# Another order for the small jobs inside an attention stage on one Trainium2 core

## What is computed

```python
x = x + 0.5 * ffn(layernorm(x))          # silu(x Wg) * (x Wu), then Wd; hidden size 768
x = x + attention(layernorm(x))          # 16 heads of 16, bias -slope * |i - j|, softmax, Wo, bo
x = x + 0.5 * ffn(layernorm(x))
```

## Time and profile before

| | |
|---|---|
| median of 3 runs | 894.81 us (894.04 to 895.18) |
| the profiled execution | 898.4 us; its span from first to last instruction 896.6 us |
| PE, PEld | busy 825.1 (92%), 503.3 us |
| DVE, ACT, POOL | busy 647.6 (72%), 522.5 (58%), 426.2 us (48%) |
| largest groups | DVE row maxima 328.5 us in 512 instructions; ACT exponentials 259.9 us in 256; POOL multiplications 186.8 us in 256 |

### The profile page before, as it was taken

The page is one execution under the profiler, slowest core; times in us unless marked ns, Lnnn a source line. Parts: engine busy times, 40 slices in busy tenths (PEclk is TensorE's granted clock), DMA queues, the critical chain, the costliest instruction groups (busy, mean ns, idle before and its releaser), DMA issues.

```text
span 896.6 us, 13035 instructions
## 1 busy us (share of the span) xinstructions
PE 825.1 (92%) x4576; PEld 503.3 (56%) x4576; DVE 647.6 (72%) x1359; ACT 522.5 (58%) x745; POOL 426.2 (48%) x486
## 2 busy tenths in 40 slices
PE   2999999858899999999999999999899987999997
PEld 2788888724354454453453444444443436888886
DVE  6898878567767777777777777776778715777764
ACT  4444434414667677777677677777577774344443
POOL 0444433422644654744644745645555545344443
PEclk9999999966999999999999999999799999999999
DMA  9320000283532532541531540540522000010001
GB/s 360 112 31 3 2 3 3 33 109 39 72 46 29 72 47 28 72 54 20 72 54 20 72 64 13 69 67 15 65 44 29 2 1 2 26 48 26 26 26 48
DMA packets 21491, 43.17 MB, mean 48 GB/s; under 512 B 3849, under 2 KB 5913, under 8 KB 21209
## 3 DMA queue, kind: packets, MB, share of 16 engines
q1 hardware_dynamic: 21400, 41.92, 27.3%
HBM read 12.02 MB, written 4.62 MB: 19 GB/s over the span
## 4 chain that ended last, share of the span: by engine, by line
PE 64%; DVE 21%; issue 4%; DMA 4%; ACT 3%; SPq 1%; POOL 1%; DVEq 0%; ACTq 0%
PE ps L938 60%; DVE row_max L859 7%; DVE hid L755 3%; DMA q_aug<-max_row 3%; PE ps L994 2%; ACT stage L612 2%; PE ps L950 1%; DVE xn L717 1%; DVE xnt L877 1%; DVE newton L694 1%; ACT xnt L618 1%; DVE var L686 1%; SPq L406 1%; DMA k_aug<-parts 1%; DVE mean_var L676 1%
## 5 line engine op out<-in xcount | busy, mean ns | idle before, releaser
L859 DVE TENSOR_REDUCE row_max<-ps 128x1 f32<-128x512 f32 x512 | 328.5, 684 | 117.6 <-PE ps L938 116.3
L650 ACT ACTIVATE probs<-ps 128x1024 f32<-128x1024 f32 x256 | 259.9, 1026 | 44.6 <-PE ps L938 44.1
L531 POOL TENSOR_TENSOR probs<-probs,diag 128x256 f32<-128x256 f32 x256 | 186.8, 734 | 199.3 <-ACT probs L650 199.1
L466 POOL TENSOR_TENSOR hid_r<-hid,hid_r 128x512 fp32r<-128x512 f32 x96 | 125.2, 1305 | 178.5 <-ACT hid_r L558 177.3
L938 PE MATMUL ps<-xnt,wgu_r 128*128 128x512 f32 x768 | 192.4, 406 | 12.1 <-DVE hid L755 7.9
L938 PE MATMUL ps<-k_aug,q_aug 60*128 60x512 f32 x512 | 171.4, 462 | 23.2 <-DVE row_max L859 10.6
L938 PEld LDWEIGHTS ps<-xnt,wgu_r 128*128 128x128 f32 x768 | 145.3, 193 | 54.0 <-DVE hid L755 14.9
L938 PE MATMUL ps<-probs,v_aug 128*32 128x512 f32 x1024 | 140.6, 622 | 6.9 <-POOL probs L531 6.9
L938 PE MATMUL ps<-q_aug,k_aug 62*128 62x512 f32 x512 | 130.9, 503 | 5.0 <-DMA q_aug<-max_row 4.6
L938 PEld LDWEIGHTS ps<-k_aug,q_aug 60*128 60x128 f32 x512 | 84.5, 195 | 81.2 <-DVE row_max L859 68.3
L564 ACT ACTIVATE gated<-ps 128x512 f32<-128x512 f32 x96 | 57.5, 599 | 121.0 <-PE ps L938 120.9
(11 more groups left out here) (63 smaller groups left out, 669.9 us busy)
## 6 DMA issues: line engine op xcount, KB each, us to landing
q_aug<-parts SPq DMA_DIRECT2D x96, 128.0 KB, 4.3
k_aug<-parts SPq DMA_DIRECT2D x96, 128.0 KB, 5.9
x_sb<-x_in SPq DMA_DIRECT2D x8, 512.0 KB, 12.8
x_out<-x_sb SPq DMA_DIRECT2D x8, 512.0 KB, 2.6
diag<-diag_table SPq DMA_DIRECT2D x1, 2048.0 KB, 18.9
wgu_i<-w_gate_up SPq DMA_DIRECT2D x2, 768.0 KB, 6.3
w_att<-w_att SPq DMA_DIRECT2D x1, 1024.0 KB, 11.7
q_aug<-max_row SPq DMA_DIRECT2D x64, 8.0 KB
```

The source lines that it names most:

```text
L466: nc.gpsimd.tensor_tensor(hid_r[:, 1, f, :], hid[:, f % 2, :], hid_r[:, 0, f, :].bitcast(F32), ALU.subtract).then_inc(s["hid_lo"], 1)
L531: nc.gpsimd.tensor_tensor(tile, tile, diag[:, kt % 2, n * QH + 2 * pair:n * QH + 2 * pair + 2, :], ALU.mult).then_inc(fixed, 1)
L650: nc.scalar.activation(probs[:, kt % 2, 2 * pair:2 * pair + 2, :], ps[:, at:at + 2, :], ACT.Exp, scale=SLOPE_UNITS[pair]).then_inc(exp_don ...
L859: nc.vector.reduce_max(row_max[:, quad % 2, u % 2, u // STEPS, (u % STEPS) // 2:(u % STEPS) // 2 + 1], max_bank(b, tile)[0], mybir.AxisLis ...
```

## The change

- In `FILLS`, every quad now has fills at steps 0, 2, 4 and 6 and "max" at step 3 (before at 0, 2, 4 and 6, and "max" at 5). Step 0 and 4 of quads 0, 1 and 3 hold a heavy one, steps 2 and 6 a light one; quad 2 holds v0, v1, heads1 and xt0.
- `xt0` and `xt1` are for sequence b + 2, at (2,6) and (3,2). Those for sequence 1 run before turn 0, ahead of the maxima. Turn 6 makes those of the last stage's first sequence, and the last turn has none.
- `turn0` is taken in the next turn (0,2), for the last sequence in the tail, which has now five fills. The two heavy fills `out0`, `out1` of the sequence before stand in quad 3.
- `MAX_LEAD` is 28.
- GpSimd's `add_bo` goes one tile at a time to steps (2,0), (2,2), (2,4), (2,6); `place_v` to (3,1), (3,3) and (3,6).
- SyncE's queue follows the new order: qk0's rows before max1, qk1 and qk2 before max2, qk3 before max3.
- The bookkeeping of counts is written anew over one list, `IN_ORDER`.

```diff
 FILLS = {
-    (0, 0): "xt0_next", (0, 2): "xt1_next", (0, 4): "heads3_prev", (0, 5): "max1", (0, 6): "qk0_next",
-    (1, 0): "qk1_next", (1, 2): "turn1_prev", (1, 4): "heads0", (1, 5): "max2", (1, 6): "out0_prev",
-    (2, 0): "out1_prev", (2, 2): "v0_next", (2, 4): "heads1", (2, 5): "max3", (2, 6): "qk2_next",
-    (3, 0): "qk3_next", (3, 2): "v1_next", (3, 4): "heads2", (3, 5): "max0_next", (3, 6): "turn0",
+    (0, 0): "qk0_next", (0, 2): "turn0_prev", (0, 3): "max1", (0, 4): "qk1_next", (0, 6): "heads3_prev",
+    (1, 0): "qk2_next", (1, 2): "turn1_prev", (1, 3): "max2", (1, 4): "qk3_next", (1, 6): "heads0",
+    (2, 0): "v0_next", (2, 2): "v1_next", (2, 3): "max3", (2, 4): "heads1", (2, 6): "xt0_next",
+    (3, 0): "out0_prev", (3, 2): "xt1_next", (3, 3): "max0_next", (3, 4): "out1_prev", (3, 6): "heads2",
 }
...
-LAST_FILLS = [f for f in ALL_FILLS if not f.endswith("_next") or f.startswith("xt")]
-TAIL_FILLS = ["heads3_prev", "turn1_prev", "out0_prev", "out1_prev"]
-
-TAIL_AT = {0: "heads3_prev", 2: "turn1_prev", 4: "out0_prev", 5: "out1_prev"}
+LAST_FILLS = [f for f in ALL_FILLS if not f.endswith("_next")]
+TAIL_FILLS = ["turn0_prev", "heads3_prev", "turn1_prev", "out0_prev", "out1_prev"]
+
+TAIL_AT = {0: "turn0_prev", 1: "heads3_prev", 3: "turn1_prev", 4: "out0_prev", 5: "out1_prev"}
...
+PLACE_AT = {(3, 1): 0, (3, 3): 1, (3, 6): 2}
 MAX_TILES = 2 * NQ * STEPS
-MAX_LEAD = 26
+MAX_LEAD = 28
...
-            seq = b + 1 if name.endswith("_next") else b - 1 if name.endswith("_prev") else b
+            ahead = 2 if name.startswith("xt") else 1
+            seq = b + ahead if name.endswith("_next") else b - 1 if name.endswith("_prev") else b
...
             for b in range(B):
+                if not last(b):
+                    wait(sp, st_done, b * (NQ * STEPS))
+                    move_rows(b, "qk0_next")
                 move_max(b, "max1")
                 if not last(b):
-                    wait(sp, st_done, b * (NQ * STEPS))
-                    for part in range(2):
-                        move_rows(b, f"qk{part}_next")
+                    move_rows(b, "qk1_next")
+                    move_rows(b, "qk2_next")
                 move_max(b, "max2")
+                if not last(b):
+                    move_rows(b, "qk3_next")
                 move_max(b, "max3")
                 if not last(b):
-                    for part in range(2, 4):
-                        move_rows(b, f"qk{part}_next")
                     move_max(b, "max0_next")
...
                         if not last(b):
-                            if (n, s) == (1, 0):
-                                add_bo(b + 1)
-                            if (n, s) == (3, 7):
-                                for quad in range(3):
-                                    place_v(b + 1, quad)
+                            if n == 2 and s % 2 == 0:
+                                add_bo(b + 1, (s // 2,))
+                            if (n, s) in PLACE_AT:
+                                place_v(b + 1, PLACE_AT[n, s])
...
             apply_kept(1, range(TT))
+            for part in range(KC):
+                split(-1, f"xt{part}_next")
             row_maxima(0, -MAX_LEAD, 0)
...
             pe.wait_ge(drained, fill_no(-1, "v1_next") + 1)
+            fill(-1, "xt0_next")
+            fill(-1, "xt1_next")
             scores_for_max(0, -MAX_LEAD, 2 * STEPS - MAX_LEAD)
```

More of the change, by code:

```diff
@@ L117 @@
 FILLS = {
[4 rows of a table removed]
[4 rows of a table added]
 }
 ALL_FILLS = list(FILLS.values())
-BANKS_BEFORE = {"qk0_next": 0, "qk1_next": 1, "v0_next": 4, "v1_next": 5, "qk2_next": 6, "qk3_next": 7, "max0_next": 7}
+BANKS_BEFORE = {"qk0_next": 0, "qk1_next": 1, "v0_next": 4, "v1_next": 5, "qk2_next": 6, "qk3_next": 7,
+                "xt0_next": 0, "xt1_next": 1, "max0_next": 7}
 FILLS_BEFORE = list(BANKS_BEFORE)
 FIRST_FILLS = [f for f in ALL_FILLS if not f.endswith("_prev")]
-LAST_FILLS = [f for f in ALL_FILLS if not f.endswith("_next") or f.startswith("xt")]
-TAIL_FILLS = ["heads3_prev", "turn1_prev", "out0_prev", "out1_prev"]
-TAIL_AT = {0: "heads3_prev", 2: "turn1_prev", 4: "out0_prev", 5: "out1_prev"}
+LAST_FILLS = [f for f in ALL_FILLS if not f.endswith("_next")]
+TAIL_FILLS = ["turn0_prev", "heads3_prev", "turn1_prev", "out0_prev", "out1_prev"]
+TAIL_AT = {0: "turn0_prev", 1: "heads3_prev", 3: "turn1_prev", 4: "out0_prev", 5: "out1_prev"}
+IN_ORDER = ([(-1, f) for f in FILLS_BEFORE] + [(0, f) for f in FIRST_FILLS] +
+            [(b, f) for b in range(1, B - 1) for f in ALL_FILLS] +
+            [(B - 1, f) for f in LAST_FILLS] + [(B, f) for f in TAIL_FILLS])
+PLACE_AT = {(3, 1): 0, (3, 3): 1, (3, 6): 2}
 MAX_TILES = 2 * NQ * STEPS
-MAX_LEAD = 26
+MAX_LEAD = 28
 SPLIT_POOL, SPLIT_DVE, HEADS, OUT = ("qk", "turn"), ("xt",), ("heads",), ("out",)
@@ L149, in count_before @@
 def count_before(b, name, kinds):
[L152 to L166, removed]
+    return len([f for _, f in IN_ORDER[:IN_ORDER.index((b, name))] if f.startswith(kinds)])
 def fill_no(b, name):
@@ L173, in slot_of @@
 def slot_of(b, name):
-    assert len([f for f in ALL_FILLS if f.startswith(STAGED)]) % 2 == 0
-    return count_before(b if isinstance(b, int) else 1, name, STAGED) % 2
+    return count_before(b, name, STAGED) % 2
 def two_before(b, name):
[L181 to L198, removed]
+    staged = [(c, f) for c, f in IN_ORDER if f.startswith(STAGED)]
+    i = staged.index((b, name))
+    return staged[i - 2] if i >= 2 else None
 def build_program(nc, d_x, d_wgu, d_wdn, d_watt, d_bo, d_qb, d_kb, d_diag, d_eye, d_scale, d_out):
@@ L508, in _, with add_bo @@
             pool.wait_ge(att_in, 16 * 2)
-            def add_bo(b):
+            def add_bo(b, tiles):
                 pool.wait_ge(xn_ready, TT * (B + b) + TT)
-                for tile in range(TT):
+                for tile in tiles:
                     nc.gpsimd.tensor_tensor(x_of(b, tile), x_of(b, tile), bo[:], ALU.add).then_inc(bo_added, 1)
-            add_bo(0)
+            add_bo(0, range(TT))
             def turn(b):
@@ L524, in turn @@
                             pool.wait_ge(pv_done, b * (NQ * TT))
-                        if (n, s) == (3, 7) and not last(b):
-                            pool.wait_ge(pv_done, b * (NQ * TT) + 3 * TT)
+                        if (n, s) in PLACE_AT and not last(b):
+                            pool.wait_ge(pv_done, b * (NQ * TT) + (PLACE_AT[n, s] + 1) * TT)
                             pool.wait_ge(drained, fill_no(b, "v1_next") + 1)
@@ L770, in ffn_turn @@
                         apply_kept(0, (2 * f, 2 * f + 1))
-                    if w == 1 and first(b) and f == 1:
-                        divide(B, TAIL_AT[0])
+                    if w == 1 and first(b) and f == 2:
+                        divide(B, TAIL_AT[1])
                 if b < B - 2:
@@ L976, in fill @@
                 elif kind == "qk":
-                    if name == "qk0_next" and not (isinstance(b, int) and b < 0):
-                        wait_done(pe, b, "xt1_next")
+                    if name == "qk0_next" and b >= 0:
+                        wait_done(pe, b - 1, "xt1_next")
                     w0 = (part % 2) * C + (part // 2) * P
@@ L996, in fill @@
                     if halves[0] == 0:
-                        wait_done(pe, b, "heads1" if part == 0 else "heads3_prev")
+                        wait_done(pe, *((seq, "heads1") if part == 0 else (b, "heads3_prev")))
                     for t in tiles:
@@ L1012, in ffn_turn @@
                 s = ffn[w]
+                if w == 1 and first(b):
+                    wait_done(pe, B - 2, "xt1_next")
                 if w == 0:
```

## The result

The changed kernel takes **922.08 us** in the median, against 894.42 for the kernel before: ratio 1.031 (95% interval 1.0284 to 1.0336). The forecast was 903.0, range 890 to 911. The direction and most of the places were right, the size was not: 27.7 us more, where I had 8.2.

The account below looks back on a forecast made before the run. The prediction took the ring of two max banks between TensorE and VectorE as the bound. Terms 4.6 + 0.4 + 4.5 + 0.5 - 2.8 + 1.0 = +8.2 on 894.8 gave 903.0 us, range 890 to 911.

Parts of the forecast that it names:

- The lead: Quads 0 and 1, step 1: GpSimd holds negate, delaying step 3; turns 67.0 against 66.1, +4.5 us for five.
- the walk: Step-by-step timing of a turn from measured matmul, reduction and fill times; gave quads of 16.6, 17.7, 15.9 and 16.8.
- the first rival (885): Quads 0 and 1: GpSimd does not hold negate, turns fall by 3.0 each, 885 us; chance 0.13.
- The front: Before turn 0: xt drains and splits delay the maxima by 3.0, two more tiles cost 1.6; +4.6 us.
- the "hidden" rival: Prologue: xt casts run before qk3's, so only the two tiles remain; 900 us, chance counted within the forecast's 0.60.
- The last turn: Last turn, without xt0, xt1 and turn0 and with out0, out1 in quad 3: -2.8 us (-5 to 0).
- SyncE's queue: qk0's six DMAs before max1, qk2's before max2: issue time hidden, no wait for the maxima.
- the clock falls more often: Rival: TensorE's new waits in step 3 of quads 0 and 1 each bring a fall of 0.9; 914 us, chance 0.12.
- Turn 0: Turn 0 has two heavy fills in quad 0 instead of one, less in quad 3: +0.4 us (-2 to +3).
- Turn 6: Turn 6, with the last stage's statistics staying in quad 1: +0.5 us by the walk.
- GpSimd's jobs: nothing: Quads 2 and 3: moved add_bo and spread place_v fit GpSimd's free 6 us, nobody waits for them; no cost.
- the tail, +1.0: Tail: turn0 adds 0.6, heads3's divide wait of 1.98 goes, out0 waits some 2; +1.0 us (-2 to +3).

Follow-up runs that it names:

- the two mended runs: Two edits of the changed kernel: MAX_LEAD 26 again, 898.86 us; GpSimd taking the low part of each qk fill one step later, 897.41 us.
- the version where VectorE takes its jobs late: Changed kernel with late qk splits, add_bo, front and tail edits, VectorE's divides and xt splits one step later: 873.82 us; out0/out1 additions also later, 871.08.
- late qk2: Changed kernel, lead 28, with only qk2's low part taken one step later on GpSimd: 905.97 us, ratio 1.0122.

## Why the prediction was wrong in its size

**What held.** *The lead.* `negate` was forecast at over 0.8 and 0.5 in step 1 of quads 0 and 1, and took 0.79 to 0.81 and 0.65 to 0.66 in turns 1 to 5. The quads were 16.6, 17.7 and 15.9 by the walk, and 16.76, 17.74 and 15.97 in turn 2; step 3 was 3.35 in quad 0 and 3.66 in quad 1 (3.40 and 3.73 by the walk). The walk with every wait gone gave 64.0 a turn; the two mended runs have 64.8 to 65.8, as quad 3 stays at 17.35 in both, where the walk had 16.8. The Trainium skill, SBUF — State Buffer, section Who interferes with whom, says that the one that is issued first keeps the shared ports for its whole instruction and the other fully blocks. The rows agree: 373.49 + 0.79 = 374.28, and the split ends at 374.25. So the first rival (885) fell. *The front*: +4.1 for +4.6; the "hidden" rival fell. Its parts held too: with the splits out of the way the first exponential is still 1.7 later than before (210.21 against 208.5), for the two tiles' 1.6. *The last turn*: -2.0 for -2.8. *SyncE's queue*: no wait for the maxima's DMA.

**Wrong: that the clock stays as before**, the largest term. Turns 1 to 5 came out 9.9 over my sum, and 5.6 of these are falls: five turns at turn 2's 67.85 would be 339.25, 346.72 - 339.25 = 7.5, and the kernel before had 1.9 of that in its two falls. The rival "the clock falls more often" had the cause and the place right, behind the waits of quad 1. But my sum kept the two falls of the earlier trace rows, and the rival took its price from them: 0.9 each, for a fall of 3.4 us. TensorE in turn 3, at half clock:

```profile
443.60 1.39 PE L916 MATMUL ps<-k_aug,q_aug 60*128 60x512 f32 x2 [0.93 <-DVE row_max L835]
444.92 1.93 PE L916 MATMUL ps<-probs,v_aug 128*32 128x512 f32 x8
```

The values take 1.93 instead of 1.07, right behind a wait of 0.93 (the clock falls 0.4 to 0.6 us after the wait's end in turns 3 and 5, 2.3 us after it in turn 4). The clock stays at 0.5 for 6.8 us and quad 1 takes 19.89 instead of 17.74: **2.2 a fall**, in turns 3, 4 and 5 (2.1 to 2.4). The argument against, that a heavy fill follows at once, did not hold: it does follow here. Turn 0, where I had +0.4 from counting fills, shows a clock of 0.86, that is 0.14 x 2 x 70.94 = 20 us at half speed, against 0.90 and 13.5 us before. At the price of turn 3 the 6.5 us more are about 2 of its +3.3, an estimate. Turn 6, where the kernel before has 10.2 us at half clock and this one 3.4, came out 2.1 under my +0.5, about the price of one long fall.

**Wrong: "GpSimd's jobs: nothing".** I looked only for who waits for GpSimd's result, not for whom its ports hold. `add_bo` holds the divide of heads1 for 0.56 (0.98 - 0.42). What that delays goes on to xt0's fill and split in the next two steps, and ends in the first step of quad 3, in turn 2:

```profile
401.98 0.69 DVE L853 TENSOR_TENSOR xnt<-stage,xnt 128x512 fp32r<-128x512 f32 x1 [1.17 <-ACT xnt L594]
...
402.29 0.51 PE L916 MATMUL ps<-q_aug,k_aug 62*128 62x512 f32 x2
...
405.98 0.50 PE L916 MATMUL ps<-q_aug,k_aug 62*128 62x512 f32 x2
```

That step takes 3.69 where the walk had 3.11, and quad 3 takes 17.38 where I had 16.8: +0.6 of the +0.85 by which turn 2 exceeds the walk. With `add_bo` a step later the step takes 3.35 and the turn 0.5 less, so `add_bo` has most of the miss. GpSimd holds `negate` of quad 3 as well:

```profile
408.05 0.74 POOL L508 TENSOR_TENSOR probs<-probs,diag 128x256 f32<-128x256 f32 x1
...
408.08 0.74 DVE L845 TENSOR_SCALAR max_in<-row_max 128x16 fp32r<-128x16 f32 x1
```

The multiplication stands there because out0's addition before it took until 408.1. But this hold costs the quad nothing: step 3 takes 2.92 for 2.65 and step 4 2.43 for 2.70, and with the lead of 26, where `negate` comes a step later and takes 0.41, quad 3 takes 17.35 all the same. (In the version where VectorE takes its jobs late, moving out0's addition as well did give 0.3.)

**Wrong: the tail, +1.0, came out +4.7.** I had let turn1's wait go, as it comes a tile later. It grew from 1.98 to 2.33, and out0 waits 2.82, where I had some 2. VectorE and GpSimd in the tail, then TensorE:

```profile
761.51 1.30 POOL L443 TENSOR_TENSOR hid_r<-hid,hid_r 128x512 fp32r<-128x512 f32 x1 [0.74 <-ACT hid_r L534]
...
761.93 0.90 DVE L670 TENSOR_TENSOR newton<-newton,var 128x4 f32<-128x4 f32 x1
...
763.38 1.26 POOL L443 TENSOR_TENSOR hid_r<-hid,hid_r 128x512 fp32r<-128x512 f32 x1 [0.57 <-ACT hid_r L534]
763.45 1.21 DVE L672 SCALAR_TENSOR_TENSOR rstd<-newton,rstd 128x4 f32<-128x4 f32 x1
...
764.85 0.42 DVE L863 TENSOR_TENSOR heads<-stage,den 128x256 f32<-128x256 f32 x1
...
765.42 1.09 PE L977 MATMUL ps<-eye,heads 128*128 128x128 f32 x4 [2.33 <-DVE heads L863]
...
772.12 1.62 PE L916 MATMUL ps<-wo,att_t 128*128 128x256 f32 x6 [2.82 <-POOL att_t L463]
```

The divide stands behind `newton` and `rstd`, four numbers a partition each, which take 0.16 when free and 0.90 and 1.21 beside `hid_r` on GpSimd: the same mechanism once more, in a place that I had not walked. What the wait would be without these holds was not tried. The wait that I had let go and the larger one make 2.33 + 0.8 of the 3.7 by which I missed. With turn1 a tile earlier the tail was 1.9 shorter, though the wait for the divide grew to 3.13.

The range of 890 to 911 held the bounds of each wait, but the clock's price only at its lowest row. It left out even that rival's own 914. At 2.2 each, the rival's twelve falls would have stood at 903 + 26 = 929; a range up to there would have held the result. Turns 1 to 6 have five falls in quads 0 and 1, not twelve: the rival's number was too high, and its price too low for the three long ones.

**Open.** Some 5 us of the medians' difference, as said; and why with the same waits the clock falls in quad 1 of turns 3 to 5, not in that of turns 1 and 2. The +3.3 of turn 0 were not taken apart by a run.

## What to carry to other kernels

A tiny VectorE instruction can take as long as what GpSimd has just begun, so before a small job is moved, look up what GpSimd runs at that moment, and look in both directions: whose result is awaited, and whose ports are held. A job that waits for a drain, at the head of an in-order queue, holds all behind it; taken one step later it was worth 12.9 us, and no data had to move. And on TensorE a new wait of under 1 us has to be priced with the clock that may fall behind it: here 0.9 for the wait, and 2.2 more in three turns of five.

## What was not expected of the hardware

- A wait of 0.92 to 0.93 on TensorE in step 3 of quad 1 was followed by 6.8 us at 0.5 of the clock in turns 3, 4 and 5; waits of 0.95 and 0.92 there, in turns 1 and 2, were not. With that wait gone (late qk2) no fall came in turns 2 to 5.
- A `negate` instruction waited for the split and the next one for the multiplication that followed it: 0.79 + 0.66 for 0.17 + 0.17 of work. GpSimd's next instruction got in between two of VectorE's.
- `RECIPROCAL` with one input of 16 numbers took 0.25 beside a multiplication on GpSimd (397.31 to 398.04, after the `add_bo` edit), its mean over all 32, while the first `negate`, also with one input of 16, was held. A multiplication with two inputs was held by `add_bo`, which began 0.03 before it.
